# Turning the normalised tokens of x1 to channels by transposing DMAs instead of TensorE transposes

## The reference

```python
x = x + experts(group_norm(x))            # 4 experts 96 -> 96 -> 96, two chosen per pixel, per image of the batch
t = tokens(x)                             # [32, 784, 96]
xh1 = (t - mean) / sqrt(var + 1e-5)       # over the 96 channels of a token
q, k, v = split(xh1 @ qkv_w + qkv_b)      # 12 heads of 8
fk, fv = fm(k), fm(v)                     # fm(t) = t + 1 if t >= 0 else exp(t)
A = fk^T fv * gauss                       # 8 x 8 per head and image
attn = A - lambda * A
t = t + (q * scale @ attn) @ proj_w + proj_b
t = t + ffn(layer_norm(t))                # sign weights, absmax quantisation over groups of 6 images, exact GELU
out = from_tokens(t)
```

## Time and profile before

| | us |
|---|---|
| median of 3 runs | 779.37 (778.01 to 780.0) |
| the profiled execution, its own time | 777.66 |
| its span, first to last instruction | 776.0 |
| TensorE busy | 727.5 |
| VectorE busy | 679.7 |
| ScalarE busy | 473.3 |
| GpSimd busy | 221.5 |
| mean granted TensorE clock | 0.977 |

### The profile page before, as it was taken

How to read it: one execution, slowest core, us unless ns; L and a number is a source line. 1 busy time by engine, 2 the same in 40 slices (tenths; PEclk the granted TensorE clock), 3 DMA queues, 4 the chain that set the end, 5 groups by cost and what they waited for, 6 DMA issues and landing times.

```text
span 776.0 us, 15540 instructions
## 1 busy us (share of the span) xinstructions
PE 727.5 (94%) x4858; PEld 480.5 (62%) x4858; DVE 679.7 (88%) x2058; ACT 473.3 (61%) x669; POOL 221.5 (29%) x301
## 2 busy tenths in 40 slices
PE   6798899999999999999999999999999899999991
PEld 3465466666766666766666766666766566555550
DVE  3577589999999999999999999999999678999997
ACT  2455356665555665555665555665554699999980
POOL 2352223324333324333324333324332001111110
PEclk8889899999999999999999999999999999999996
DMA  9970111111111111111111111111110101564446
GB/s 216 199 186 1 32 33 32 34 47 31 31 47 31 31 47 31 31 47 31 31 47 31 31 47 31 31 47 31 31 31 16 31 1 19 91 127 60 62 63 140
DMA packets 17663, 41.40 MB, mean 53 GB/s; under 512 B 4553, under 2 KB 4839, under 8 KB 17639
## 3 DMA queue, kind: packets, MB, share of 16 engines
q1 hardware_dynamic: 14552, 33.27, 16.4%
q0 software_dynamic: 2688, 7.23, 6.6%
q10 hardware_dynamic: 399, 0.60, 0.3%
HBM read 22.28 MB, written 18.67 MB: 53 GB/s over the span
## 4 chain that ended last, share of the span: by engine, by line
PE 63%; DVE 18%; issue 6%; ACT 5%; SPq 3%; DMA 2%; POOL 2%; DVEq 1%; ACTq 0%; POOLq 0%
PE slot L1071 15%; PE slot L1055 13%; PE slot L1284 6%; PE slot L1077 5%; PE slot L917 5%; PE slot L1082 5%; PE slot L1131 5%; DVE stage L1659 4%; PE slot L1118 4%; ACT stage L799 4%; SPq L476 3%; DVE stage L1646 3%; DVE y2max L1765 2%; DVE xn L1788 1%; PE slot L1342 1%
## 5 line engine op out<-in xcount | busy, mean ns | idle before, releaser
L1071 PE MATMUL slot<-hT,w2s 128*96 128x392 f32 x372 | 132.6, 492 | 0.8 <-DVE w2s L1532 0.8
L1613 DVE TENSOR_SCALAR tok<-tok,ln_mv,ln_rs 112x96 f32<-112x96 f32 x434 | 109.0, 322 | 2.0 <-POOL ln_rs L624 1.9
L624 POOL TENSOR_TENSOR ln_rs<-ln_ve,pow_half 112x7 f32<-112x7 f32 (+2 forms) x92 | 105.1, 1142 | 7.2
L799 ACT ACTIVATE stage<-slot,kv_bias,kv_unit 112x768 f32<-112x768 f32 (+1 forms) x62 | 53.1, 907 | 86.6 <-PE slot L1118 86.6
L621 POOL TENSOR_TENSOR ln_ve<-ln_mv,ln_eps 112x7 f32<-112x7 f32 (+2 forms) x92 | 18.3, 199 | 296.1 <-DVE ln_mv L1595 296.1
L792 ACT ACTIVATE hT<-slot,b1c,w_unit 128x784 f32<-128x784 f32 x93 | 93.1, 1004 | 15.8 <-PE slot L1055 13.2
L1082 PE MATMUL slot<-big,W1b 96*128 (+1 forms) x360 | 89.3, 329 | 0.0
L1071 PEld LDWEIGHTS slot<-hT,w2s 128*96 128x96 f32 x372 | 58.6, 163 | 45.0 <-issue 42.9
L1619 DVE TENSOR_REDUCE ymax<-slot 128x784 f32 (+1 forms) x90 | 84.5, 966 | 0.0
L1077 PE MATMUL slot<-big,W1b 99*128 (+1 forms) x360 | 84.4, 329 | 0.0
L854 ACT ACTIVATE hT<-slot,s 128x784 f32<-128x784 f32 x90 | 80.2, 914 | 6.1 <-DVE stage L1646 3.2
(11 more groups left out here) (252 smaller groups left out, 1455.4 us busy)
## 6 DMA issues: line engine op xcount, KB each, us to landing
xs<-in_x SPq DMA_DIRECT2D x32, 294.0 KB, 2.9
out<-h_second SPq DMA_DIRECT2D x32, 294.0 KB, 2.6
big<-in_x SPq DMA_DIRECT2D x7, 1176.0 KB, 15.5
out<-h_second POOLq DMA_DIRECT2D x24, 294.0 KB, 4.2
big<-out SPq DMA_DIRECT2D x1, 1764.0 KB, 10.5
out<-big SPq DMA_DIRECT2D x6, 294.0 KB, 2.7
big<-in_x SPq DMA_DIRECT2D x2, 588.0 KB, 24.5
con<-shape_consts ACTq DMA_DIRECT2D x1, 445.5 KB, 6.3
```

The source lines that it names most:

```text
L624: nc.gpsimd.tensor_tensor(ln_rs[n][:, j0:j1], ln_ve[n][:, j0:j1], pow_half[0:TOK, j0:j1], ALU.pow).then_inc(ln_rstd[part], 1)
L799: nc.scalar.activation(ekv[:, j0:j0 + n, :], chunks(k, n, 256, 2 * C), ACT.Exp, bias=kv_bias[:, :], scale=kv_unit[0:TOK, 0:1]).then_inc(e_ ...
L1071: ins = mm(S[k][0:C, h, 0:HALF], w2s[:, v, t, :], src[:, t, h * HALF:(h + 1) * HALF], start=t == 0, stop=t == last, skip_group_check=True)
L1613: ins = V.tensor_scalar(src[:, j, :], src[:, j, :], ln_mv[n][:, j, 0:1], ln_rs[n][:, j:j + 1], ALU.subtract, ALU.mult)
```

## The change

The tokens of x1 are split into float16 parts while they are still tokens: ScalarE casts `tok1` to `x1_hi` and VectorE subtracts, `x1_lo`, both in SBUF. Each part is padded from 96 to 128 columns; the pads are zero, and one of ones in the high part becomes the row for the bias. SP issues two transposing DMAs per image, high and low, that write `xh1_hi` and `xh1_lo` by channels. TensorE's transposes of x1 fall away, and `kv` waits for the two DMAs.

With it, some orders change. On ScalarE the cast of x1 stands ahead of the third Relu. On VectorE the low part stands between the first four statistics of x2 and their moments. SP does the transposes of a step ahead of the load and the store of that step, and its loop is written out. In `last_attend` and in the second step there are more `keep_busy` matmuls. The new tiles take their SBUF from set-up weights that are dead by then (`by_channel`), and GpSimd fills the pads once, after the set-up.

```diff
+        by_channel = sb("by_channel", [P, 3 * HID])
...
+        x1_lo = token_part(by_channel[0:TOK, 0:TOKENS])
+        x1_hi = sb("x1_hi", [TOK, CHUNKS, P], F16)
...
-        xh1_hi = sb("xh1_hi", [C + 1, HW + P - TOK], F16)
-        xh1_lo = sb("xh1_lo", [C, HW + P - TOK], F16)
+        xh1_hi = sb("xh1_hi", [P, HW + P - TOK], F16)
+        xh1_lo = sb("xh1_lo", [P, HW + P - TOK], F16)
...
+            def move_x1(i):
+                sp.wait_ge(x1_hi_ready, i)
+                if isinstance(i, int) and i == 1:
+                    sp.wait_ge(pads_ready, 1)
+                else:
+                    sp.wait_ge(ao_ready, i - 1)
+                sp.dma_start_transpose(turned(xh1_hi[:, 0:HW]),
+                                       x1_hi[:, :, :].rearrange("p j c -> p (j c)")).then_inc(x1_hi_moved, 16)
+                sp.wait_ge(x1_lo_ready, i)
+                sp.dma_start_transpose(turned(xh1_lo[:, 0:HW]),
+                                       x1_lo[:, :, :].rearrange("p j c -> p (j c)")).then_inc(x1_lo_moved, 16)
...
-            with sp.Fori(FIRST // 2, LAST // 2 - 1) as m:
+            for m in range(FIRST // 2, LAST // 2 - 1):
                 for r in range(2):
+                    move_x1(2 * m + r)
                     load_next(m, r)
                     store_last(m, r)
             for r in range(2):
+                move_x1(LAST - 2 + r)
                 store_last(LAST // 2 - 1, r)
+            move_x1(LAST)
             store_last(LAST // 2, 0)
...
+            pool.wait_ge(kvw_ready, 2)
+            pool.wait_ge(setup_T, 1)
+            pool.wait_ge(bigones_ready, 16)
+            then(nc.gpsimd.memset(x1_lo[:, :, C:P], 0.0))
+            then(nc.gpsimd.memset(x1_hi[:, :, C:P], 0.0))
+            nc.gpsimd.memset(x1_hi[:, :, C:C + 1], 1.0).then_inc(pads_ready, 1)
...
-            def xh1_high(i):
-                act.wait_ge(x1T_ready, i)
-                nc.scalar.copy(*channels(xh1_hi[0:C, 0:HW], 0)).then_inc(xh1_hi_ready, 1)
+            def x1_high(i):
+                act.wait_ge(xh1_ready, i)
+                nc.scalar.copy(x1_hi[:, :, 0:C], tok1[:, :, :]).then_inc(x1_hi_ready, 1)
...
+                if attend:
+                    x1_high(i)
                 if experts and not between and not early:
                     relu(2, 2)
                 if attend:
-                    xh1_high(i)
                     exp_kv(0, 3, 0, CH_A)
...
-                pe.wait_ge(xh1_lo_ready, done)
+                pe.wait_ge(x1_lo_moved, 16 * done)
                 kv_part(k, j0, n, xh1_lo, kvw_hi[0:C, :], False).then_inc(kv_ready, 1)
...
-                pe.wait_ge(xh1_ready, BATCH)
-                to_channels(0, tok1, x1T_ready)
                 y1_max_row()
-                keep_busy(1, 0, 2)
-                pe.wait_ge(xh1_hi_ready, BATCH)
+                keep_busy(1, 0, 12)
+                pe.wait_ge(x1_hi_moved, 16 * BATCH)
...
-                if attend and not second:
-                    x1_to_channels()
...
                 if second:
                     keep_busy(0, 0, 4)
-                    x1_to_channels()
                     pe.wait_ge(gate_exp_in, 3)
-                    keep_busy(2, 0, 4)
+                    keep_busy(2, 0, 8)
                 if attend:
-                    pe.wait_ge(xh1_hi_ready, i)
+                    pe.wait_ge(x1_hi_moved, 16 * i)
...
-            def stats2(f):
+            def stats2(f, between):
                 chunk_stats(tok2, range(CH_A)).then_inc(ln_stats[1], 1)
+                between()
+                moments(1, f + 1)
                 chunk_stats(tok2, range(CH_A, CH_A + 1))
-                moments(1, f + 1)
                 chunk_stats(tok2, range(CH_A + 1, CHUNKS)).then_inc(ln_stats[2], 1)
                 moments(2, f + 1)
...
+                def x1_low():
+                    if attend:
+                        dve.wait_ge(x1_hi_ready, i)
+                        V.tensor_tensor(x1_lo[:, :, 0:C], tok1[:, :, :], x1_hi[:, :, 0:C],
+                                        ALU.subtract).then_inc(x1_lo_ready, 1)
+
                 if ffn:
                     dve.wait_ge(tok2_ready, f + 1)
-                    stats2(f)
-                if attend:
-                    dve.wait_ge(xh1_hi_ready, i)
-                    V.tensor_tensor(tokenwise(xh1_lo[:, 0:HW]),
-                                    flat(0)[0:C, 0:CHUNKS * P].rearrange("p (j t) -> p j t", t=P)[:, :, 0:TOK],
-                                    tokenwise(xh1_hi[0:C, 0:HW]), ALU.subtract).then_inc(xh1_lo_ready, 1)
+                    stats2(f, x1_low)
```

More of the change, by code:

```diff
@@ L159, in build, with token_part @@
         ident = con[:, K_ID:K_ID + P]
-        w1_raw = sb("w1_raw", [P, TILES, C])
-        w2_raw = sb("w2_raw", [C, E, C])
+        by_channel = sb("by_channel", [P, 3 * HID])
+        w2_raw = by_channel[0:C, 0:HID].rearrange("p (e d) -> p e d", e=E)
+        W2_raw = by_channel[0:C, HID:2 * HID]
+        part_b = by_channel[:, 2 * HID:3 * HID]
+        by_row = sb("by_row", [P, 2, TILES, C])
+        w1_raw = by_row[:, 0, :, :]
+        W1_raw = by_row[:, 1, :, :]
+        TOKENS = CHUNKS * P // 2
+        def token_part(view):
+            return view.bitcast(F16).rearrange("p (j c) -> p j c", c=P)
+        x1_lo = token_part(by_channel[0:TOK, 0:TOKENS])
+        x1_hi = sb("x1_hi", [TOK, CHUNKS, P], F16)
         w1_max = sb("w1_max", [P, TILES])
@@ L384, in build @@
         xh2_ready = sem("xh2_ready")
-        x1T_ready = sem("x1T_ready")
-        xh1_hi_ready = sem("xh1_hi_ready")
-        xh1_lo_ready = sem("xh1_lo_ready")
+        x1_hi_ready = sem("x1_hi_ready")
+        x1_lo_ready = sem("x1_lo_ready")
+        x1_hi_moved = sem("x1_hi_moved")
+        x1_lo_moved = sem("x1_lo_moved")
+        pads_ready = sem("pads_ready")
         w_max_ready = sem("w_max_ready")
@@ L494, in _, with turned @@
                 sp.dma_start(xs[r][:, :], x_bcn[r]).then_inc(xs_loaded[r], 16)
+            def turned(dst):
+                return dst.rearrange("p (j t) -> p j t", t=TOK)
+            def move_x1(i):
[9 more added lines that the diff above has]
+                                       x1_lo[:, :, :].rearrange("p j c -> p (j c)")).then_inc(x1_lo_moved, 16)
             def load_next(m, r):
@@ L506, in _ @@
                 for r in range(2):
+                    if m + r > 0:
+                        move_x1(2 * m + r)
                     load_next(m, r)
```

22 lines of the change are left out of this document (10 added, 12 removed).

## The result

| | before | after |
|---|---|---|
| median of 4 runs, us | 778.69 (776.81 to 780.0) | 796.08 (793.48 to 799.23) |
| ratio of the medians, 95% interval | | 1.0227 (1.0182 to 1.0272) |
| profiled execution, its own time / span | 777.66 / 776.0 | 793.48 / 791.8 |
| mean granted TensorE clock | 0.977 | 0.971 |

The change makes the kernel slower, by 17.4 us. The forecast was 785, its range 770 to 812: the sign was right and the size, 6.1 us, was about a third of what came. The busy line of the page shows nothing of this: TensorE is busy 3.6 us less than in the earlier trace rows, VectorE the same.

The account below looks back on a forecast made before the run. TensorE (94% busy) and VectorE (88%) were taken as close bounds, VectorE taking over the loop. +3.2 us (loop) and +2.9 (last step) made +6.1, 783.8 for the profiled execution; forecast 785, range 770 to 812.

Parts of the forecast that it names:

- The bound: In the loop, VectorE takes over at once: of TensorE's removed 0.67 us a step only 0.05 us stay.
- ScalarE, VectorE, GpSimd: In a step: cast about 0.75 us, low part 0.85, GpSimd's power exposed before the apply of x2, t1 at 311.74.
- Rival C: Faster: VectorE's subtraction from SBUF runs at about twice the rate, 0.45 us for 0.85; 769 or 774 us; chance 0.20.
- The time to landing: Each transposing DMA lands 2.9 us after issue, as the dearer plain copy does, between bounds of 2.0 and 5.8.
- the hold of SP's queue: Each transposing DMA was taken to hold SP's queue as a plain copy does, 0.34 us.
- the steady loop: Low part lands at 311.24, so the feature map starts 0.11 us later a step: 29 x 0.11 = +3.2 us.
- hand-over of 0.17 us: SP issues a DMA 0.17 us behind the engine it waits for, so the low part goes out at 308.34.
- VectorE's deadline of 311.08: Low part's latest landing for VectorE's feature map start at 312.69, a time to landing of 2.74 us.
- Rival D: Much slower: each transpose holds SP's queue far longer than 0.34 us, deciding above 0.5; 809 or 845 us; chance 0.21.
- The last step: The last image's transposes stand behind the store of t2; low products start at 610.08 instead of 607.13: +2.9 us.
- The second step: Idle time everywhere; low matmuls start at 93.99 against 93.98, so no cost.
- SP's program: Writing out SP's loop costs only instruction loading; nothing was added to the sum.

Follow-up runs that it names:

- v2_pe_back: The changed kernel with the seven TensorE transposes of x1 put back, their result unread: 795.19 us, 1.0216 against the kernel before.
- v1_no_low: The changed kernel without the transposing DMA of the low part, the low products reading zeros: 783.1 us, 1.0061 against the kernel before.
- v3_last_first: The changed kernel with the last image's two transposes ahead of the store of image 30 on SP's queue: 794.0 us, 1.0207 against the kernel before.
- v8_best: The changed kernel with the low DMA in four and three chunks, low part behind x2's first moments, last image's transposes ahead of the store: 789.88 us, 1.0166.
- v5_moments_first: The changed kernel with the low part of x1 behind the first moments of x2 instead of ahead: 797.8 us, 1.0242 against the kernel before.

## Why the prediction was right in sign and short in size

**The bound.** Right. TensorE's 0.67 us were worth nothing (`v2_pe_back`), and VectorE, waiting for GpSimd's power, takes the step over at 16.55 (`v1_no_low`), where the working gave 16.64 - 0.05 = 16.59.

**ScalarE, VectorE, GpSimd.** Right to 0.03 us. With 3.81 taken off, the cast ends at 307.30 (307.29 forecast) and takes 0.75, the low part 0.86 (0.85) and ends at 308.19 (308.17), t1 starts at 311.72 (311.74); VectorE waits 0.48 us for the power. Rival C is out: the subtraction from SBUF has no faster rate. The rule of the Trainium skill that was held against C ("VectorE: DVE Perf Modes", "Why `tensor_tensor` can't do 2×_2P or 4×" and the table ahead of it), one result a cycle, fits the trace: between 96 elements (0.26 us) and 672 (0.86) an element costs 1.04 ns, as from PSUM in the earlier trace rows (1.03) and not half of it.

**The time to landing.** 2.9 forecast from a plain copy, 2.84 measured. The Trainium skill's 1309 ns for one block ("VectorE: DVE Perf Modes", "The three transpose paths") would be 9.2 us for seven one behind another, an estimate; nothing in the traces is near it.

**The step that failed is the hold of SP's queue.** The sum took a copy's 0.34 us, with which the low part finds the queue free and goes out at 308.34. The hold is 1.21 us, and it went out at 312.39 - 3.81 = 308.58, 0.24 later; less 0.06 for the quicker landing that is 0.18 to 0.19 a step, 29 x 0.19 = 5.5, which is all of the 5.2 us by which the steady loop (8.4) passed its term (3.2). The sum's hand-over of 0.17 us hid a part of it: a free SP took 0.02 to 0.04. With a copy's hold, the low part, complete at 308.19, would have gone out at about 308.22 and landed by 311.06, inside VectorE's deadline of 311.08, an estimate from these rows; so the hold is the whole loss of the loop. Rival D had named this hold, but its price was wrong: it added the hold to the 2.56 us that a copy needs behind its own, which would give a landing 3.8 us behind issue. In fact only 2.84 - 1.29 = 1.55 us come behind the low part's own hold. So the point from which the hold costs was not D's 0.5 us either, but the time between the two parts, 312.03 - 311.13 = 0.90 us. The forecast had a landing as long as a copy's and D a hold far above a copy's, as alternatives, and both were true. A long hold inside an unchanged landing was no case of the sum. That 796 lies inside the range of 770 to 812 is owed to the room left for D, not to a case that was worked out.

**The last step.** Mechanism right, size 6.6 for 2.9 us; the difference has three parts. Counted from the last t1, the high products start at 16.26 where 15.2 was worked out, +1.05: the high part goes out 0.1 us later and lands in 3.84 us, not 2.9. The high products run slow, +0.3. And from the low products to the end the kernel loses another 2.2 us, at the start of which the clock is at its lower level for 6 us. "The twelve fillers cover part of the idle time and cost nothing" was the sentence that failed: 2.34 us of waiting were left behind them, and the clock fell. `v3_last_first`, and `v8_best` with the same order, show in the rows that the order on the queue brings most of the wait, and with it the fall: 0.63 us of waiting in both. It doesn't show that the store makes the landing long, since that stays at 3.86 us without it.

**The second step and the set-up.** Nothing was forecast for the second step, +1.0 came. Its low part took 1.58 us beside work of GpSimd, and the stretch 96 to 104 was granted 0.84 where before it had 1.00. No run undid these alone. For the pads and the shared SBUF of the set-up the sum had nothing, or 1 us if GpSimd's cover was gone. The set-up is 1.0 us longer in the mean of the profiled executions (81.4 for 80.4), with a wide spread; its cause is open.

**SP's program.** "That SP's loop is written out costs only instruction loading" put a term at nothing. Five profiled executions of kernels with transposes have one long step at the start of the loop that the kernel before has not (19.36 us in `v5_moments_first`, 19.23 in `v8_best`, 18.89 in `v2_pe_back`, 18.33 in `v1_no_low`, 17.84 in `v3_last_first`, none in the profiled execution of the kernel after). In each of the five a transpose just ahead of it or in it lands late with a code transfer beside it: 4.0 us (`v5_moments_first`), 3.9, 4.7, 4.3 and 4.3, for 2.8. These steps and the set-up fit the wider spread of the times after, 793 to 799. Whose code it is the view doesn't say, and no run keeps SP's loop short, so whether writing it out brings them stays open.

## What to carry to other kernels

Cost a DMA by two prices, the time to landing and the time that its queue is held. When two transfers stand one behind the other on one queue and the second is on the path, what counts is the part of the first one's hold that is left when the second is ready (0.35 of 1.21 us here), and cutting a transfer in pieces is a gain only while the pieces' holds stay off the path (788 us with the low part cut, 855 with both cut, the second also by a fall of the clock in many of its steps). And before work is moved from the engine with the most busy time, ask what the next engine's step would be: here 0.67 us removed brought 0.09 even where no low part was moved.

## What the runs showed of the hardware

- A transposing DMA within SBUF, issued by SP, holds the queue 1.19 to 1.33 us in the steady loop, with 1, 3, 4, 6, 7 or 9 chunks of 112 x 128 elements of 16 bits; a plain copy of 294 KB 0.33 us.
- It lands 2.3 us behind its issue with one chunk, 2.3 to 2.5 with three or four, 2.7 to 2.9 with seven, 3.1 with nine. With a transfer of program code beside it, seven chunks took 3.86 us with no store in front (`v3_last_first`), 3.84 right behind a store of 294 KB (the kernel after) and 4.0 in the loop (`v5_moments_first`). The Trainium skill, "Advanced Engine Details and Errata", section "X-Bar Transpose (TRN2)", calls such DMAs as fast as regular ones: for the landing the trace agrees (2.84 against 2.6 and 2.9), for the hold it doesn't.
- Beside a VectorE subtraction of two SBUF tiles, a GpSimd addition of 112 x 4 took 0.72 us for 0.20.
- Behind a wait of 2.34 us TensorE's granted clock was at its lower level from about 620.2 to 627.0 us, and a pair of matmuls took 0.86 us for 0.50. Behind a wait of 2.19 us in another execution it stayed at 1.00 for 7 us and fell later. With the wait down to 0.63 us (`v3_last_first`) it was 1.00 from 618 to 632 us.
